# Second attention with two sets of buffers and its rolls in a row; MLP that rounds a pair behind the next pair's shrinking

## The chip, the cores and the metric

The kernel runs on one core of a Trainium2 chip. The metric is the device time of one execution in microseconds (us), median of three runs. TensorE is called PE below, VectorE DVE, ScalarE ACT, GpSimd POOL, and SyncE, which issues all transfers here, SP.

## What is computed

Two layers on `x` (32 batches x 64 tokens x 128), with `ctx` of the same shape as context. Each layer adds a gated attention and a gated MLP to the residual, each behind a layer norm. `setup_inputs` draws everything in float32.

```python
x = x + tanh(g_xattn[0]) * attention0(_layernorm(x), ctx)    # rope, 16 heads of 8, softmax
x = x + tanh(g_ffn[0]) * experts(_layernorm(x))              # 8 experts, top 2 for each batch of (8, 256), gelu
x = x + tanh(g_xattn[1]) * autocorrelation(_layernorm(x), ctx)
x = x + tanh(g_ffn[1]) * fp4_mlp(_layernorm(x))

# autocorrelation, for each batch
Q, K, V = (query @ Wq + bq), (key @ Wk + bk), (value @ Wv + bv)       # split in heads
corr = irfft(rfft(Q) * conj(rfft(K)))
w, idx = top_k(corr.mean(axis=-1), 4)                                 # the best four lags of a head
out = sum over the four: softmax(w) * V rolled by idx                 # then @ Wo + bo

# fp4_mlp: blocks of 16 are scaled by max(abs)/6, rounded to the fp4 grid, scaled back
h = silu(fp4_linear(x, w_gate)) * fp4_linear(x, w_up)                 # 352 wide
return fp4_linear(h, w_down)                                          # quantises h and w_down too
```

## The kernel before, in words

**Tiling.** `x` stays in SBUF as 16 tiles (`TILES`) of 128 rows (two batches) x 128 columns. A group is four tiles, so there are four groups (`G4`); a pair is two tiles, so there are eight pairs (`PAIRS`). All intermediate data lies in one large SBUF tensor, `region`, which every stage carves anew, so in the trace nearly every operand is called `s_region`. PSUM is one tensor `ps` of eight banks.

**What sets the order.** There is no scheduler. Each engine has one hand-written list of calls (`@block.vector` and its fellows), and semaphores, named in `names`, make it wait. The order of work on an engine is the order of the calls in the text, and an instruction that waits holds everything behind it on its engine.

**Stages.** The first attention runs to about 93 us; routing and experts follow to 171 us; the second attention to its last residual add at 214 us, with its output product, the layer norm and the first quantisation to 229 us; the MLP then runs to 291.5 us. `keep_clock(n, bank)` (L1107) is `n` matmuls on PE whose result nobody reads.

**First attention.** For each tile, `keys_queries` makes the scores of two banks, `row_max` and `subtract` on DVE (L733, L741) and the exponent on ACT (L511) make the probabilities, PE turns them (L1143), ACT copies them (L516), PE multiplies by the values (L1156). A product of the output bias (PE L1197 and L1198, then DVE L764 into `bout`) stands between the loads of the pipeline and its loop.

**Second attention.** Two halves `k` of 16 batches each. Their heads' products of spectra (`products`, DVE L908) are summed by PE into bank 4 + k (`sum_heads`, L1363), copied by ACT (`sums_read`, L597), turned by PE (`turn_sums`, L1374), copied by ACT (`sums_turned`, L603), and transformed back by PE (`correlate`, L1382). DVE finds the best lags (`best_lags`, L910 to L929, with an exponent on ACT, L607, in its midst), PE turns them (`turn_lags`, L1413), ACT spreads them over the heads (`turn_gx`, L614). For each pair of tiles, PE makes the spectrum of the roll (`spectrum`, L1424), and DVE multiplies it with the spectrum of the values (`roll_values`, L938). `context_kv(n)` (L1244, with a small bias product L1230) projects keys (n below 4) and values (n from 4); ACT copies them (L534). `cfs`, `cfT`, `gx`, `y1` and the bank of the correlation have one buffer each, so the second half waits for the first at each of them. Spectra use two banks:

```python
if q >= 2:
    pe.wait_ge(m["of_done"], 2 * (q - 1))
```

`out_product` (L1432), `y1_turned` (ACT L619), `out_tokens` (L1439) and `attention_out` (DVE L969) end the stage for each group; `turn_weights` (PE L1324, L1328; copy ACT L587) turns the quantised weights of the MLP in between.

**MLP.** A group of `x` is quantised in five steps: `x_scale` (DVE: reduce, scale, reciprocal, shrink, L268 to L270 and L275), `x_magnitude` (ACT L667), `x_round` (DVE L279, twice), `x_unscale` (POOL L286, 512 columns), `turn_x` (PE L1472) with its copy (ACT L650). A pair then goes through `gate_up` (PE L1485), `silu` (ACT L655), the product `hh` (DVE L995), reduce (L1005), scale (L1010), reciprocal (L1011), shrink (L275), `magnitude` (ACT L661), the rounding (DVE L279, 704 columns, twice), the unscaling (POOL L286, 704 columns), `turn_h` (PE L1499), its copy to `hT` (ACT L688), `down` (PE L1509) and `finish` (DVE L1017, the residual add). In `pair_step(q)` DVE does the product of pair q, the rounding of pair q-1, the reduce of pair q, `finish(q - 3)`, then scale, reciprocal and shrink of pair q. PE's loop is:

```python
for q in range(PAIRS + 2):
    if q + 1 < PAIRS:
        gate_up(q + 1)
    if q >= 2:
        down(q - 2)
    if 1 <= q <= PAIRS:
        turn_h(q - 1)
```

with `turn_x` at its end for q of 0, 2 and 4.

## Time and profile before

| what | us |
|---|---|
| median of three runs (297.94 to 299.8) | 299.23 |
| the profiled execution, its own time | 295.81 |
| its span in the trace | 293.8 |
| outside the span (the difference) | 2.0 |

The profile is of one execution. Its span is the time from the first to the last recorded instruction or transfer; the device time holds some 2.0 us more. A row of a timeline gives the start, the duration, the engine, the line, the operation, what it writes and reads, the shape, how many instructions the row stands for, and in brackets how long the engine had been idle before and what released it. The granted clock of PE is given as a share of its full speed (in the 40 slices in tenths, in the windows as a mean).

### The profile page before, as it was taken

Reading aid. Unit: us, or ns where it says so; the run is one execution under the profiler, and the core shown is the slowest. Engines: PE = TensorE matmul, PEld = TensorE weight load, DVE = VectorE, ACT = ScalarE, POOL = GpSimd, SP = SyncE. Lnnn points to the kernel's source line nnn. Section 1 sums busy time; section 2 is a strip of 40 time slices with the busy share of each in tenths; the row PEclk is TensorE's granted clock in tenths of the full one; section 3 lists DMA queues with packets and bytes.
Section 4 is the critical chain, followed back from the end, with each engine's and each line's share of the span. In section 5 each row is a group of like instructions: output and inputs, shape, how many; then the busy total and the mean of one; then the engine's idle time right before and its main releaser. Section 6 shows DMA issues by size and latency. Waiting matters only on the chain.

```text
span 293.8 us, 6298 instructions
## 1 busy us (share of the span) xinstructions
PE 261.2 (89%) x2190; PEld 203.5 (69%) x2190; DVE 199.5 (68%) x538; ACT 161.4 (55%) x368; POOL 120.8 (41%) x172
## 2 busy tenths in 40 slices
PE   8999899999899999999999998987857869696955
PEld 5655466666578789999999975554645547374855
DVE  3997588889987744322222269746287999998981
ACT  2579975555786666666666647224443824443421
POOL 4573879995203042299522015302253131313121
PEclk9999999999999999999999999999998969797999
DMA  7997000000001197767777300000000000000001
GB/s 204 370 363 316 3 2 0 2 2 2 2 3 20 73 379 325 294 287 288 288 289 300 134 0 2 1 3 0 0 0 0 2 1 0 18 19 19 18 19 56
DMA packets 12159, 30.15 MB, mean 103 GB/s; under 512 B 992, under 2 KB 5216, under 8 KB 12000
## 3 DMA queue, kind: packets, MB, share of 16 engines
q1 hardware_dynamic: 12128, 29.75, 26.8%
q8 instruction: 18, 0.29, 0.4%
q14 instruction: 13, 0.11, 0.1%
HBM read 9.75 MB, written 1.05 MB: 37 GB/s over the span
## 4 chain that ended last, share of the span: by engine, by line
PE 63%; DVE 17%; ACT 7%; issue 5%; POOL 3%; DMA 2%; SPq 1%; DVEq 0%; ACTq 0%; POOLq 0%
PE ps L1307 11%; PE ps L1296 11%; PE ps L1156 5%; PE ps L1130 4%; PE ps L1485 4%; PE ps L1143 4%; DVE s_region L279 4%; PE ps L1058 3%; PE ps L1424 3%; PE ps L1049 2%; DVE s_small L228 2%; PE ps L1166 2%; PE ps L1050 2%; DVE s_region L995 2%; DVE s_small L1005 1%
## 5 line engine op out<-in xcount | busy, mean ns | idle before, releaser
L573 ACT ACTIVATE s_region<-ps,s_region 128x128 f32<-128x128 f32 x144 | 41.1, 369 | 22.0 <-PE ps L1296 21.8
L868 DVE SCALAR_TENSOR_TENSOR s_ctxT<-ps,s_region,s_ctxT 128x64 f32 x72 | 18.1, 282 | 44.3 <-PE ps L1307 44.2
L1296 PE MATMUL ps<-s_region 128*128 128x128 f32 x288 | 38.5, 276 | 0.3
L1307 PE MATMUL ps<-s_region 128*128 128x128 f32 x288 | 37.9, 275 | 0.0
L286 POOL TENSOR_TENSOR s_region<-s_region,s_small 128x704 f32<-128x704 f32 (+2 forms) x13 | 17.5, 1343 | 46.5 <-DVE s_region L279 46.5
L1296 PEld LDWEIGHTS ps<-s_region 128*128 128x128 f32 x288 | 35.0, 192 | 1.0 <-DMA s_region<-s_wall 0.6
L1307 PEld LDWEIGHTS ps<-s_region 128*128 128x128 f32 x288 | 35.0, 192 | 0.2 <-issue 0.2
L251 POOL TENSOR_TENSOR s_small<-s_small,s_par 128x4 f32<-128x4 f32 (+3 forms) x14 | 15.5, 1107 | 43.2 <-DVE s_small L234 43.2
L1485 PE MATMUL ps<-s_region 128*128 128x352 f32 x64 | 26.4, 570 | 2.3 <-ACT s_region L650 2.3
L398 POOL COPY s_region<-s_xt 128x64 f32 x72 | 14.8, 238 | 32.1 <-PE ps L1296 22.0
L733 DVE TENSOR_REDUCE s_small<-ps 128x16 f32<-128x1024 f32 x16 | 19.6, 1225 | 9.9 <-PE ps L1130 9.9
L516 ACT COPY s_region<-ps 128x512 f32<-128x512 f32 x32 | 17.2, 588 | 16.3 <-PE ps L1143 16.2
L345 POOL TENSOR_SCALAR s_region<-s_region 128x512 f32<-128x512 f32 x16 | 24.7, 1572 | 2.1 <-PE ps L1130 2.1
L242 ACT ACTIVATE s_xn<-s_x,s_small 128x128 f32<-128x128 f32 x47 | 19.5, 485 | 5.4 <-POOL s_small L253 5.3
L279 DVE SCALAR_TENSOR_TENSOR s_region<-s_region 128x704 f32<-128x704 f32 (+1 forms) x24 | 20.6, 859 | 2.6 <-ACT s_region L667 1.2
L1485 PEld LDWEIGHTS ps<-s_region 128*128 128x128 f32 x64 | 14.2, 234 | 11.0 <-issue 4.0
L741 DVE TENSOR_TENSOR s_region<-ps,s_small 128x1024 f32<-128x1024 f32 x16 | 18.7, 1171 | 0.0
L1156 PEld LDWEIGHTS ps<-s_region 128*64 128x64 f32 x512 | 16.2, 138 | 3.1 <-ACT s_region L516 1.5
L1156 PE MATMUL ps<-s_region 128*64 128x18 f32 x512 | 17.8, 212 | 0.3 <-ACT s_region L516 0.2
L511 ACT ACTIVATE s_region<-s_region 128x1024 f32<-128x1024 f32 x16 | 17.1, 1068 | 1.3 <-DVE s_region L741 1.2
L1130 PE MATMUL ps<-s_region 64*64 64x512 f32 x128 | 17.4, 614 | 0.0
L1143 PE MATMUL ps<-s_par,s_region 128*128 128x128 f32 x128 | 16.6, 273 | 0.0
(216 smaller groups left out, 509.0 us busy)
## 6 DMA issues: line engine op xcount, KB each, us to landing
s_region<-s_wall SPq DMA_DIRECT2D x36, 514.0 KB, 3.0
s_wall<-wall SPq DMA_DIRECT2D x8, 514.0 KB, 9.0
s_par<-par SPq DMA_DIRECT2D x1, 1316.0 KB, 10.5
s_x<-x SPq DMA_DIRECT2D x2, 512.0 KB, 6.8
out<-s_x SPq DMA_DIRECT2D x8, 128.0 KB, 1.8
s_region<-ffn SPq DMA_DIRECT2D x1, 560.0 KB, 3.6
s_ctxT<-ctxT SPq DMA_DIRECT2D x2, 256.0 KB, 4.2
s_ctxT<-ctxT SPq DMA_DIRECT2D x1, 512.0 KB, 6.7
```

Of the source, the lines that this page charges most:

```text
L242: ins = eng.activation(xn[:, t, :], x[:, t, :], ACT.Identity, bias=shift[:, t:t + 1], scale=rstd[:, t:t + 1])
L279: return eng.scalar_tensor_tensor(out, mag, 1.5, z, ALU.max, ALU.subtract)
L345: pool.tensor_scalar(kbd[g % 2][:, j, :], cols, hmask[:, j:j + 1], None, ALU.mult).then_inc(m["kbd_done"], 1)
L573: ins = act.activation(hg[j % 3][:, c, :], ps[:, j % 3, RPT * S * c:RPT * S * (c + 1)], ACT.Gelu, bias=wbuf[j % 6][:, FF + FC * D + c:FF + ...
L733: dve.tensor_reduce(mx[t % 2], scores(t % 2), AX, ALU.max).then_inc(m["mx_done"], 1)
L741: dve.tensor_tensor(ssub[t % 2], scores(t % 2), mx[t % 2].unsqueeze(2).broadcast_to([P, H, S]), ALU.subtract).then_inc(m["s_sub"], 1)
L1130: ins = mm(ps[S * row:S * row + S, 2 * (t % 2) + half, :], qT[rows, 2 * t + row, :], kbd[g % 2][rows, :, k:k + S], start=True, stop=True)
L1143: ins = tr(ps[:, 4 + half, P * k:P * k + P], pr[t % 2][:, c:c + P], ident)
L1156: ins = mm(ps[S * row:S * row + S, 6 + t % 2, n * c:n * c + n], pT[t % 2][:, c, S * row:S * row + S], vbd[:, 2 * t + row, c, :], start=Tru ...
L1296: ins = mm(ps[:, j % 3, RPT * S * c:RPT * S * (c + 1)], w[:, P * c:P * c + P], xg[j % 4], start=True, stop=True)
L1307: ins = mm(ps[:, 4 + j % 2, 0:RPT * S], w[:, FF + D * c:FF + D * c + D], hg[j % 3][:, c, :], start=(c == 0), stop=(c == FC - 1))
L1485: ins = mm(ps[:, 1 + 2 * n + t, 0:MLP], xqT[(q // 2) % 2][:, lo:lo + P], wguT[:, MT * P * n:MT * P * n + MLP], start=True, stop=True)
```

## The change

**First attention.** The two matmuls of the bias product move on PE from ahead of the first turning of probabilities to a place behind the keys and queries of tile 2, and DVE's `bout` from ahead of `subtract(1)` to behind `row_max(2)`.

**Second attention.** `cfs`, `cfT`, `gx` and `y1` get a second buffer, the correlation a bank for each half (7 - k); turned sums and lags go to bank 4 + k. Spectra use four banks, so roll q waits for roll q-4. PE has both halves' sums, turns and correlations in a row; the values' projections 4 and 5 stand earlier (where `keep_clock` stood twice), 6 and 7 behind both correlations. `queries(3)` stands ahead of `sum_heads(0)`, `products(3)` ahead of the last two bias adds on DVE. ACT's order follows. POOL normalises two tiles of the last group and ACT two, instead of POOL four. The output product and the weights are turned at other places among the spectra.

**MLP.** DVE's `pair_step(q)` does product, reduce, `finish(q - 3)`, scale, reciprocal and shrink of pair q, and only then the rounding of pair q-1. PE's loop is now `down(q - 3)`, `gate_up(q + 1)`, `turn_h(q - 2)`, `turn_x`. ACT copies `hT` of pair q-2, where it was q-1. `finish` of the last three pairs stands behind the loop.

```diff
+KV_BANK = (6, 7, 6, 7, 6, 7, 2, 3)
+SPEC_BANK = (0, 1, 6, 7)
...
+        cfs = [carve(18432, 4, P), carve(8192, 4, P)]
+        cfT = [carve(18944 + 256 * i, 2, P) for i in range(2)]
...
+        gx = [carve(26880, TILES // 2, H, HD), carve(16384, TILES // 2, H, HD)]
...
+        y1 = [carve(27904, 4, P), carve(25600, 4, P)]
...
             sums_read(0)
+            sums_read(1)
             sums_turned(0)
-            kv_turned(4)
+            sums_turned(1)
             exp_lead(0)
-            sums_read(1)
-            sums_turned(1)
+            kv_turned(6)
             turn_gx(0)
-            kv_turned(5)
             exp_lead(1)
-            kv_turned(6)
+            kv_turned(7)
             turn_gx(1)
-            kv_turned(7)
...
-                if q >= 1:
-                    act.wait_ge(m["ht_done"], q)
-                    act.copy(hT[(q - 1) % 2].rearrange("p a k b -> p a (k b)"), ps[:, 5:7, 0:MT * P]).then_inc(m["ht_used"], 1)
+                if q >= 2:
+                    act.wait_ge(m["ht_done"], q - 1)
+                    act.copy(hT[q % 2].rearrange("p a k b -> p a (k b)"), ps[:, 5:7, 0:MT * P]).then_inc(m["ht_used"], 1)
...
             products(2)
+            products(3)
             bias_added(2)
             bias_added(3)
-            products(3)
...
-                if second:
-                    dve.wait_ge(m["hm_done"], q)
-                    dd.step(fp4_off(dve, hd[w], hm[w], hh[w].rearrange("p a n -> p (a n)")))
-                    fp4_off(dve, hd[w], hm[w], hd[w]).then_inc(m["hd_done"], 1)
-                if first:
...
-                if q >= 3:
-                    finish(q - 3)
-                if first:
+                    if q >= 3:
+                        finish(q - 3)
                     dd.after(k)
...
                     fp4_shrunk(dve, blocks(flat), blocks(flat), spread(hin[n3], 2 * NH)).then_inc(m["hv_done"], 1)
+                if 1 <= q <= PAIRS:
+                    dve.wait_ge(m["hm_done"], q)
+                    if q >= 3:
+                        dve.wait_ge(m["hq_done"], q - 2)
+                    dd.step(fp4_off(dve, hd[w], hm[w], hh[w].rearrange("p a n -> p (a n)")))
+                    fp4_off(dve, hd[w], hm[w], hd[w]).then_inc(m["hd_done"], 1)
...
-            keep_clock(4, 1)
+            context_kv(4)
             turn_experts(3)
             to_frequency(0)
-            keep_clock(3, 3)
+            context_kv(5)
...
+            queries(3)
             sum_heads(0)
-            queries(3)
-            context_kv(4)
+            sum_heads(1)
             turn_sums(0)
-            sum_heads(1)
+            turn_sums(1)
             correlate(0)
-            context_kv(5)
-            turn_sums(1)
             correlate(1)
+            context_kv(6)
+            context_kv(7)
...
-                if q >= 2:
-                    pe.wait_ge(m["of_done"], 2 * (q - 1))
+                if q >= 4:
+                    pe.wait_ge(m["of_done"], 2 * (q - 3))
+                elif q >= 2:
+                    pe.wait_ge(m["corr_read"], 2)
+                else:
+                    pe.wait_ge(m["pp_done"], 2 * G4)
...
-            for q in range(PAIRS + 2):
+            for q in range(PAIRS + 3):
+                if q >= 3:
+                    down(q - 3)
                 if q + 1 < PAIRS:
                     gate_up(q + 1)
-                if q >= 2:
-                    down(q - 2)
-                if 1 <= q <= PAIRS:
-                    turn_h(q - 1)
+                if 2 <= q <= PAIRS + 1:
+                    turn_h(q - 2)
+                if q in (0, 2, 4):
+                    turn_x(q // 2 + 1)
```

PE's order in the second attention, from the first turned lags on. L1413 turns lags, L1424 is a spectrum, L1244 with L1230 a projection of values. Before:

```order
L1413 MATMUL ps<-s_par,s_region 128x128 [waits hs_read,lags_ready]
L1424 MATMUL ps<-s_par,s_region 128x256 [waits gx_ready]
L1424 MATMUL ps<-s_par,s_region 128x256
L1424 MATMUL ps<-s_par,s_region 128x256 [waits gx_ready]
L1424 MATMUL ps<-s_par,s_region 128x256
L1413 MATMUL ps<-s_par,s_region 128x128 [waits cf_ready,lags_ready]
L1244 MATMUL ps<-s_region,s_par 128x512 [waits kv_used,cf_used]
L1230 MATMUL ps<-s_small,s_par 128x8 [waits bias64_ready]
L1424 MATMUL ps<-s_par,s_region 128x256 [waits of_done,gx_ready]
L1424 MATMUL ps<-s_par,s_region 128x256
L1424 MATMUL ps<-s_par,s_region 128x256 [waits of_done,gx_ready]
L1424 MATMUL ps<-s_par,s_region 128x256
```

The same place now (L1422 turns lags, L1437 is a spectrum, L1334 turns weights):

```order
L1422 MATMUL ps<-s_par,s_region 128x128 [waits cf_ready,lags_ready]
L1437 MATMUL ps<-s_par,s_region 128x256 [waits pp_done,gx_ready]
L1437 MATMUL ps<-s_par,s_region 128x256
L1437 MATMUL ps<-s_par,s_region 128x256 [waits pp_done,gx_ready]
L1437 MATMUL ps<-s_par,s_region 128x256
L1422 MATMUL ps<-s_par,s_region 128x128 [waits cf_ready,lags_ready]
L1437 MATMUL ps<-s_par,s_region 128x256 [waits corr_read,gx_ready]
L1437 MATMUL ps<-s_par,s_region 128x256
L1437 MATMUL ps<-s_par,s_region 128x256 [waits corr_read,gx_ready]
L1437 MATMUL ps<-s_par,s_region 128x256
L1334 MATMUL ps<-s_par,s_region 128x128 [waits kv_used,wq_ready]
```

The last projection of values is gone from between the spectra, and the third and fourth spectrum wait for `corr_read` (DVE has copied the second correlation) where they waited for `of_done` (DVE has multiplied the roll two before).

DVE's order in the MLP, `pair_step(3)` and the `x_scale(3)` behind it. L995 is the product, L279 with 704 columns the rounding of pair 2, L1005 the reduce, L1017 `finish(0)`, L275 a shrink. Before:

```order
L995 TENSOR_TENSOR s_region<-s_region,ps 128x704
L279 SCALAR_TENSOR_TENSOR s_region<-s_region 128x704 x2
L1005 TENSOR_REDUCE s_small<-s_region 128x44
L1017 SCALAR_TENSOR_TENSOR s_x<-ps,s_small,s_x 128x256
L1010 TENSOR_SCALAR s_small<-s_small 128x44
L1011 RECIPROCAL s_small<-s_small 128x44
L275 SCALAR_TENSOR_TENSOR s_region<-s_region,s_small 128x704
L268 TENSOR_REDUCE s_small<-s_xn 128x32
```

Now, from the end of `pair_step(2)` and the `x_round(2)` behind it to the same `x_scale(3)` (L999 is the product, L281 the rounding, L1004 the reduce, L1021 `finish`, L277 the shrink, L270 the first step of `x_scale`):

```order
L281 SCALAR_TENSOR_TENSOR s_region<-s_region 128x704 x2
L281 SCALAR_TENSOR_TENSOR s_region<-s_region 128x512 x2
L999 TENSOR_TENSOR s_region<-s_region,ps 128x704
L1004 TENSOR_REDUCE s_small<-s_region 128x44
L1021 SCALAR_TENSOR_TENSOR s_x<-ps,s_small,s_x 128x256
L1008 TENSOR_SCALAR s_small<-s_small 128x44
L1009 RECIPROCAL s_small<-s_small 128x44
L277 SCALAR_TENSOR_TENSOR s_region<-s_region,s_small 128x704
L281 SCALAR_TENSOR_TENSOR s_region<-s_region 128x704 x2
L270 TENSOR_REDUCE s_small<-s_xn 128x32
```

Between the product and `finish` there were three instructions and there is one; a rounding of 704 columns now stands directly ahead of each `x_round` (512 columns) and each `x_scale`.

PE's order in the MLP around the `turn_x(3)` (L1472) of loop step 4. L1485 is `gate_up`, L1509 `down`, L1499 `turn_h`. Before:

```order
L1509 MATMUL ps<-s_region 128x128 x6
L1499 MATMUL ps<-s_par,s_region 128x128 x2
L1499 MATMUL ps<-s_par,s_region 96x128
L1499 MATMUL ps<-s_par,s_region 128x128 x2
L1499 MATMUL ps<-s_par,s_region 96x128
L1472 MATMUL ps<-s_par,s_region 128x128 x4
L1485 MATMUL ps<-s_region 128x352 x4
L1509 MATMUL ps<-s_region 128x128 x6
```

The same place now (L1482 is `turn_x`, L1519 `down`, L1495 `gate_up`, L1509 `turn_h`):

```order
L1509 MATMUL ps<-s_par,s_region 128x128 x2
L1509 MATMUL ps<-s_par,s_region 96x128
L1509 MATMUL ps<-s_par,s_region 128x128 x2
L1509 MATMUL ps<-s_par,s_region 96x128
L1482 MATMUL ps<-s_par,s_region 128x128 x4
L1519 MATMUL ps<-s_region 128x128 x6
L1495 MATMUL ps<-s_region 128x352 x4
```

Behind `turn_x` comes `down` first and then `gate_up`, where `down` followed `gate_up`.

## Rows read from the trace of the kernel before

**Rows 1.** The page: busy time of each engine.

```profile
PE 261.2 (89%) x2190; PEld 203.5 (69%) x2190; DVE 199.5 (68%) x538; ACT 161.4 (55%) x368; POOL 120.8 (41%) x172
```

**Rows 2.** Windows in the MLP: length, busy PE, PEld, DVE, ACT, POOL; clock, DMA.

```profile
229.00:243.00 14.00, 10.66 (x35) 6.60 (x34) 13.25 (x22) 7.03 (x13) 3.50 (x4) 0.78 0.01 2
...
257.00:271.00 14.00, 11.18 (x56) 8.07 (x55) 13.45 (x21) 5.11 (x9) 3.84 (x3) 0.87 0.07 20
```

**Rows 3.** Timeline of DVE in the second attention, where it waits.

```profile
193.26 0.29 DVE L913 COPY s_region<-ps 128x128 f32<-128x128 f32 x1 [2.14 <-PE ps L1382]
...
197.45 0.29 DVE L913 COPY s_region<-ps 128x128 f32<-128x128 f32 x1 [1.47 <-PE ps L1382]
...
200.41 0.29 DVE L924 SCALAR_TENSOR_TENSOR s_region<-s_region 128x128 f32<-128x128 f32 x1 [1.41 <-ACT s_region L607]
...
204.00 1.62 DVE L938 TENSOR_TENSOR s_region<-ps,s_region 128x256 f32<-128x256 f32 x4 [1.12 <-PE ps L1424]
207.15 1.62 DVE L938 TENSOR_TENSOR s_region<-ps,s_region 128x256 f32<-128x256 f32 x4 [1.53 <-PE ps L1424]
212.61 1.62 DVE L938 TENSOR_TENSOR s_region<-ps,s_region 128x256 f32<-128x256 f32 x4 [3.84 <-PE ps L1424]
```

**Rows 4.** Timelines of ACT and PE at the lags of the second half.

```profile
204.85 1.01 ACT L614 COPY s_region<-ps 128x1024 f32<-128x1024 f32 x1 [4.07 <-PE ps L1424]
...
202.78 1.97 PE L1424 MATMUL ps<-s_par,s_region 128*128 128x256 f32 x8
```

**Rows 5.** Timeline of DVE in the MLP: two pairs whole, and single rows around.

```profile
232.75 0.19 DVE L1010 TENSOR_SCALAR s_small<-s_small 128x44 f32<-128x44 f32 x1
...
249.24 1.41 DVE L279 SCALAR_TENSOR_TENSOR s_region<-s_region 128x512 f32<-128x512 f32 x2
250.57 0.88 DVE L995 TENSOR_TENSOR s_region<-s_region,ps 128x704 f32<-128x704 f32 x1
251.37 2.10 DVE L279 SCALAR_TENSOR_TENSOR s_region<-s_region 128x704 f32<-128x704 f32 x2
...
254.18 0.47 DVE L1017 SCALAR_TENSOR_TENSOR s_x<-ps,s_small,s_x 128x256 f32<-128x256 f32 x1
254.57 0.40 DVE L1010 TENSOR_SCALAR s_small<-s_small 128x44 f32<-128x44 f32 x1
...
259.01 1.81 DVE L279 SCALAR_TENSOR_TENSOR s_region<-s_region 128x704 f32<-128x704 f32 x2
...
264.97 0.88 DVE L995 TENSOR_TENSOR s_region<-s_region,ps 128x704 f32<-128x704 f32 x1
...
271.97 0.89 DVE L995 TENSOR_TENSOR s_region<-s_region,ps 128x704 f32<-128x704 f32 x1 [1.21 <-PE ps L1485]
...
283.92 1.82 DVE L279 SCALAR_TENSOR_TENSOR s_region<-s_region 128x704 f32<-128x704 f32 x2 [0.86 <-ACT s_region L661]
```

**Rows 6.** Timeline of POOL beside them.

```profile
250.73 1.06 POOL L286 TENSOR_TENSOR s_region<-s_region,s_small 128x512 f32<-128x512 f32 x1 [2.84 <-DVE s_region L279]
253.54 1.39 POOL L286 TENSOR_TENSOR s_region<-s_region,s_small 128x704 f32<-128x704 f32 x1 [1.75 <-DVE s_region L279]
```

**Rows 7.** Timeline of PE in the MLP.

```profile
245.12 2.53 PE L1485 MATMUL ps<-s_region 128*128 128x352 f32 x8
247.49 1.50 PE L1509 MATMUL ps<-s_region 128*128 128x128 f32 x12
...
251.85 0.66 PE L1472 MATMUL ps<-s_par,s_region 128*128 128x128 f32 x4 [2.20 <-POOL s_region L286]
253.18 4.33 PE L1485 MATMUL ps<-s_region 128*128 128x352 f32 x8 [0.68 <-ACT s_region L650]
```

**Rows 8.** Timeline of ACT in the MLP: the copy to `hT`, and `x_magnitude`.

```profile
250.06 0.78 ACT L688 COPY s_region<-ps 128x768 f32<-128x768 f32 x1
...
258.33 0.63 ACT L667 ACTIVATE s_region<-s_region 128x512 f32<-128x512 f32 x1 [1.14 <-DVE s_region L275]
```

**Rows 9.** Timeline of DVE in the first attention.

```profile
33.86 0.35 DVE L764 TENSOR_SCALAR s_region<-ps,s_small 128x128 f32<-128x128 f32 x1 [0.60 <-PE ps L1198]
```

More of the change, by code:

```diff
@@ L678, in _ @@
             normalise(act, 12, 16, m["xn_d"], 14)
-            for q in range(PAIRS + 1):
+            for q in range(PAIRS + 2):
                 if q + 1 < PAIRS:
@@ L990, in pair_step @@
                 u, w, n3 = q % 2, (q - 1) % 2, q % 3
-                first, second = q < PAIRS, 1 <= q <= PAIRS
-                if first:
+                if q < PAIRS:
                     dve.wait_ge(m["sg_done"], q + 1)
@@ L1029, in _ @@
             x_scale(1)
-            for q in range(PAIRS + 3):
+            for q in range(PAIRS + 1):
                 pair_step(q)
@@ L1035, in _ @@
                     x_scale((q + 3) // 2)
+            for q in range(PAIRS - 3, PAIRS):
+                finish(q)
         @block.tensor
@@ L1202, in _ @@
                     keys_queries(t + 2)
+                if t == 0:
+                    bias_product()
                 if t >= 1:
@@ L1525, in _ @@
                     keep_clock(9 if q == PAIRS - 2 else 3, 0)
-                if q in (0, 2, 4):
-                    turn_x(q // 2 + 1)
 def _constants():
```

107 lines of the change are left out of this document (52 added, 55 removed).

## The prediction

> **What bounds the kernel now.** I read the busy time of the engines first, then timelines of one engine after the other in the two stages that the change touches, then windows for the clock. PE is busy for 89% of the span and DVE for 68% [rows 1], but a share over the whole span says little: each stage has its own limit.
>
> In the second attention the thing to see is that DVE, at the end of the chain, waits six times: 2.14 and 1.47 us for the two correlations, 1.41 us for an exponent on ACT, and 1.12, 1.53 and 3.84 us for spectra [rows 3]. The last comes from one buffer: ACT's spreading of the second half's lags waits 4.07 us for the first half's spectra to be read, and PE's four spectra for it start only then [rows 4]. Latency bounds this stage, and buffers cause much of it.
>
> In the MLP the reverse holds. From the product at 250.57 to the one at 264.97, two pairs and 14.40 us, DVE has no gap [rows 5]; it is busy for 13.45 of 14 us while PE is busy for 11.18 [rows 2]. DVE bounds it. Two details matter. PE waits 2.20 us for POOL at L1472 and 0.68 us more for ACT, and then its `gate_up` takes 4.33 us where it takes 2.53 at other times [rows 7]; the granted clock over such stretches is 0.78 and 0.87 [rows 2], so part of them ran at 1.2 GHz and not 2.4, after a wait. DVE hides that today, with only 1.21 us of wait at one product [rows 5]. And POOL's unscaling of a pair takes 1.39 us and ends at 254.93; DVE's tiny L1010 began at 254.57 and ended at 254.97, taking 0.40 us where it takes 0.19 with POOL idle; the rounding beside POOL's other unscaling took 2.10 us, not 1.81 [rows 5, 6]. DVE and POOL get in each other's way.
>
> **First attention.** The bias product leaves the place ahead of the second subtraction. DVE waited 0.60 us and worked 0.35 us for it there [rows 9]; moved one tile later, its product is long there. PE does both matmuls anyway. What can come out is at most about 0.5 us and at least 0 (if PE, which does the same work, bounds the loop); I take -0.25, near L764's own time.
>
> **Second attention.** The removed and the shortened waits, one by one. The first correlation: both halves' sums now stand ahead of it on PE, but the bias adds leave DVE's path; I take no gain, since they cancel by about 1 us each. The second correlation comes right behind the first, so its 1.47 us go. The exponent is asked for earlier and stands only behind one spreading of 1.01 us: of 1.41 us about 0.4 stay, -1.0. The rolls' 1.12 + 1.53 + 3.84 = 6.49 us shrink, because four banks let PE run ahead and the second `gx` has its own buffer. What stays is PE's pace: four spectra for two rolls, 1.97 us [rows 4], against 1.62 us of DVE [rows 3], four times, some 0.35 x 4 = 1.4, and 0.3 for the first; about 1.7 stay, -4.8. Sum -1.5 - 1.0 - 4.8 = -7.3. The output products and weight turns now lie between the spectra, and the first tokens are ready a bit later relative to the last roll: +0.8, an estimate out of PE's order. Net -6.5. From both sides: none of the rolls' gain would leave -1.7, and every one of the six waits gone would be -11.5; the value is nearest to the rows that one buffer explains.
>
> **MLP, per two pairs.** The new order has DVE do product, reduce, `finish`, scale, reciprocal, shrink of pair q and only then the rounding of q-1. No instruction is added or dropped. Terms for the cycle of 14.40 us [rows 5]:
>
> - DVE and POOL meet elsewhere. The L1010 of both pairs get 0.40 - 0.19 = 0.21 us back, and one rounding 2.10 - 1.81 = 0.29: -0.71.
> - POOL's unscaling of 1.39 us [rows 6] starts when a rounding ends, and the next on DVE is now an `x_round` or an `x_scale`. The first instruction of an `x_round` (half of 1.41 us, rows 5) starts at once, its second has to wait for what remains of the 1.39: I take +1.3; behind `x_scale`, whose first instruction reads one buffer, the scaling of the middle is late by about half of POOL's time, +0.7. The bounds are 0 (they pass each other, as the product and POOL's 512-column unscaling of 1.06 us do [rows 5, 6]) and 1.39 each.
> - `finish(q - 3)` waits for `down(q - 3)`. It is still in the same place, but `down` now is issued an iteration later and `hT` is copied an iteration later, so `finish` has only the product and the reduce ahead of it, some 1.7 us. For even pairs `down` (1.50 us, rows 7) stands on PE behind `turn_x`, which waits for POOL's 1.06 behind POOL's 1.39 [rows 6]; then 1.06 + 0.66 + 1.50 = 3.2 us stand against that cover of 1.7: +1.5. For odd pairs ACT's copy of 0.78 us stands behind `x_magnitude` of 0.63 us [rows 8]; 0.63 + 0.78 + 1.50 = 2.9 against 1.7: +1.25. The bounds are 0 (down is issued in time) and 3.2 each.
>
> Sum 14.40 - 0.71 + 2.0 + 2.75 = 18.4, that is +4.0 per two pairs. It applies once in full, for the pairs 3 and 4. Pairs 0 to 2 have no `finish` yet: of the above only the meeting with POOL, +0.7. Pairs 5 and 6 have no `x_scale`, and the wait of 1.21 us at their product [rows 5] covers part: 2.75 - 1.21 - 0.42 = +1.1. For pair 7 and the end there are two waits of about 1.3, less the 0.86 us that DVE stood for ACT's magnitude [rows 5] and that a rounding now covers, less 0.2 at L1010: +1.5. After the last rounding the chain is the same as before. Sum 0.7 + 4.0 + 1.1 + 1.5 = +7.3.
>
> What is queued behind a waiting `finish`: scale, reciprocal and shrink of pair q on DVE, so ACT's magnitude, and the rounding of q-1, so POOL, `turn_h` and the next `down`. It is a loop: a late `down` makes the next one late. This is why the waits add up.
>
> The Trainium skill, page "SBUF — State Buffer", section "SBUF: two separate sides", states that the port pair DVE and GpSimd share is an exclusive lock, held for a whole instruction by whoever starts first, where DVE's instruction has two SBUF inputs and GpSimd's reads SBUF. The trace agrees: L1010 ended 0.04 us behind POOL's 1.39 us. By that rule the second half of `x_round` and of the later roundings meets a lock held since a rounding ended, as in the term above, and speaks against this order; by the reading that they pass each other the sum would be 2.0 us lower in the full cycle.
>
> **The clock.** PE's waits in the MLP are 2.20 + 0.68 us before a slow `gate_up` [rows 7]. In the new order `turn_x` waits for both unscalings and `down` for `finish`, so I estimate waits of 4 to 5 us. A slow `gate_up` costs 4.33 - 2.53 = 1.80 us and a slow `down` as much as it lasts, 1.5. Before, DVE hid it; now `down` and `gate_up` stand on the path. One and a half such misses is +2.5; the bounds are 0 and, for three slow `gate_up` with nothing to hide them, 3 x 1.80 = 5.4. The Trainium skill, page "TensorE: Matmul & The Clock Gate", section "HAM oscillation — how this bites in real kernels", says that waits between groups of matmuls put TensorE back to half its clock each time, so that every group starts cold; that is the third rival below. By that rule each `turn_x` wait here costs a slow `gate_up`, as the trace shows after 2.20 us already.
>
> **Sum.** -0.25 - 6.5 + 7.3 + 2.5 = +3.05. The profiled execution took 295.81 us, of which 293.8 are its span and 2.0 lie outside, which nothing here changes: 295.81 + 3.05 = 298.86. The median of the runs is 299.23, 3.42 above the profiled one, so 302.3 on its scale.
>
> **Rivals.**
>
> - An even exchange: the attention gives 6.75 and the MLP takes 7.3, but the clock is as before. Speaks for it: most of PE's work is the same, only in another order, and PE waited before too. Against: its waits grow. +0.55, 299.8.
> - The rolls' gain stands and `finish` never waits: faster. The mechanism is in one place, L1017: `down(q - 3)` stands first in PE's loop, and if PE comes to it while DVE still does the shrink of the pair before, `dn_done` is there when DVE asks. It decides when `turn_h` and its copy are done before the product of pair q. Then in the MLP only the meeting with POOL stays, 0.7 + 2.0 - 0.71, less the freed 1.21 and 0.86: about -0.1, and the time is 299.23 - 6.75 - 0.1 = 292.4. For it: DVE has no gap now at any L1017 in the two pairs [rows 5]. Against: the cover is 1.7 us where a rounding of 1.81 to 2.10 us more stood before.
> - The clock stays low over most of the MLP: the clock term is 5.4 + 0.4 for the first `gate_up` and not 2.5, +3.3 more, 305.6. For it: 0.78 in the first stretch [rows 2].
> - The rolls don't run in a row: the copies of the last values (ACT) or the exponent hold the second `gx`, and the attention gives only 3.3: 302.3 + 3.2 = 305.5. Against: ACT waits 4.07 us there and has room [rows 4].
>
> **How the numbers follow.** The forecast 0.42, the even exchange 0.22, the faster case 0.14, the low clock 0.14, the rolls 0.08. About 1%, 3 us, is what a measurement of this kernel can tell from no change. The forecast, at +3.1, lies on the bound and is split between slower and same, 0.25 and 0.17; the even exchange is same but for 0.02 faster; the two last are slower. Slower 0.25 + 0.14 + 0.08 = 0.47, same 0.17 + 0.20 = 0.37, faster 0.14 + 0.02 = 0.16. The range leaves out most of the faster case. Its low end is the forecast without the clock term (2.5), without the meetings with POOL (2.7) and without 1.7 of the waits, 295.4; its high end is the case of the low clock, 305.6, with 1.4 us more of waits for `down`, 307.0. The forecast's own range is 300 to 305.
>
> **What would show it.** In the profile after: the copy of the second correlation (L913 of before) without a wait, four rows of rolls with waits under 1 us, the last rolls some 7 us earlier than 212.61 [rows 3]; in the MLP, waits of 1 to 1.5 us at the `finish` on PE's `down`, an `x_round` of about 2.5 us where it is 1.41, and windows with a clock under 0.87. Wrong would be: no wait at `finish`; products in the MLP 14.4 us apart per two pairs; or a clock of 1.00.

## The result

The changed kernel takes 302.25 us (median of 4 runs, 302.03 to 302.51) against 299.47 us for the kernel before in the same measurement: ratio 1.0139, 95% interval 1.0089 to 1.019. A second measurement on another occasion gave 301.27 against 297.49 us, ratio 1.0131 (1.0071 to 1.0192). It is slower by somewhat over 1%: 2.8 us in the first measurement and 3.8 in the second, where +3.05 was forecast.

The profiled execution after took 302.03 us, its span is 299.9. Its page:

```profile
PE 261.0 (87%) x2176; PEld 205.0 (68%) x2176; DVE 201.9 (67%) x538; ACT 162.2 (54%) x370; POOL 120.6 (40%) x170
```

Only DVE is busy for longer than before, 201.9 us where it was 199.5 [rows 1]; the others are within 1.5 us. Most of the 6.1 us by which the span grew is waits. The clearest reading is by three marks: the first residual add of layer 1 (L896 before, L899 after), the last roll, and the first product of the MLP, with the end of the last residual add. Timeline of DVE, these marks before (the last roll stands in [rows 3]):

```profile
172.67 0.75 DVE L896 SCALAR_TENSOR_TENSOR s_x<-ps,s_small,s_x 128x512 f32<-128x512 f32 x1 [0.84 <-PE ps L1336]
...
230.91 0.89 DVE L995 TENSOR_TENSOR s_region<-s_region,ps 128x704 f32<-128x704 f32 x1 [0.23 <-PE ps L1485]
...
291.04 0.48 DVE L1017 SCALAR_TENSOR_TENSOR s_x<-ps,s_small,s_x 128x256 f32<-128x256 f32 x1 [2.67 <-PE ps L1509]
```

And after (the last roll and the first product stand in the next fence):

```profile
174.21 0.75 DVE L899 SCALAR_TENSOR_TENSOR s_x<-ps,s_small,s_x 128x512 f32<-128x512 f32 x1 [0.84 <-PE ps L1346]
...
297.17 0.48 DVE L1021 SCALAR_TENSOR_TENSOR s_x<-ps,s_small,s_x 128x256 f32<-128x256 f32 x1 [2.67 <-PE ps L1519]
```

| | first add | last roll | first product | end of last add | MLP's length |
|---|---|---|---|---|---|
| before | 172.67 | 212.61 | 230.91 | 291.52 | 60.6 |
| after | 174.21 | 207.14 | 228.25 | 297.65 | 69.4 |
| difference | +1.5 | -5.5 | -2.7 | +6.1 | +8.8 |

So up to the first add 1.5 us are lost, from there to the last roll 7.0 are won, from the last roll to the first product 2.8 are given back, and in the MLP 8.8 are lost.

**Second attention.** Timeline of DVE, the rows that answer to [rows 3], and the first product:

```profile
195.18 0.29 DVE L916 COPY s_region<-ps 128x128 f32<-128x128 f32 x1 [2.39 <-PE ps L1391]
...
197.82 0.28 DVE L916 COPY s_region<-ps 128x128 f32<-128x128 f32 x1
...
199.65 0.29 DVE L927 SCALAR_TENSOR_TENSOR s_region<-s_region 128x128 f32<-128x128 f32 x1 [0.30 <-ACT s_region L605]
...
202.46 1.62 DVE L941 TENSOR_TENSOR s_region<-ps,s_region 128x256 f32<-128x256 f32 x4 [0.22 <-PE ps L1437]
204.52 1.62 DVE L941 TENSOR_TENSOR s_region<-ps,s_region 128x256 f32<-128x256 f32 x4 [0.44 <-PE ps L1437]
207.14 1.62 DVE L941 TENSOR_TENSOR s_region<-ps,s_region 128x256 f32<-128x256 f32 x4 [1.00 <-PE ps L1437]
...
228.25 0.89 DVE L999 TENSOR_TENSOR s_region<-s_region,ps 128x704 f32<-128x704 f32 x1 [1.04 <-PE ps L1495]
```

The second correlation waits for nothing, the exponent's wait is 0.30 where it was 1.41, and the rolls' waits are 0.22, 0.44 and 1.00, together 1.66 where they were 6.49. This is the forecast for these waits one by one (0, 0.4, 1.7).

**MLP.** Timeline of DVE, pairs 3 to 5 and the wait of pair 7, which answers to [rows 5]:

```profile
238.69 0.87 DVE L271 TENSOR_SCALAR s_small<-s_small 128x32 f32<-128x32 f32 x1
...
243.93 4.21 DVE L281 SCALAR_TENSOR_TENSOR s_region<-s_region 128x704 f32<-128x704 f32 x4
248.05 0.87 DVE L999 TENSOR_TENSOR s_region<-s_region,ps 128x704 f32<-128x704 f32 x1
249.03 0.89 DVE L1004 TENSOR_REDUCE s_small<-s_region 128x44 f32<-128x704 f32 x1
253.03 0.48 DVE L1021 SCALAR_TENSOR_TENSOR s_x<-ps,s_small,s_x 128x256 f32<-128x256 f32 x1 [3.12 <-PE ps L1519]
...
262.91 0.48 DVE L1021 SCALAR_TENSOR_TENSOR s_x<-ps,s_small,s_x 128x256 f32<-128x256 f32 x1 [1.77 <-PE ps L1519]
...
268.93 0.88 DVE L999 TENSOR_TENSOR s_region<-s_region,ps 128x704 f32<-128x704 f32 x1
...
272.23 0.48 DVE L1021 SCALAR_TENSOR_TENSOR s_x<-ps,s_small,s_x 128x256 f32<-128x256 f32 x1 [1.44 <-PE ps L1519]
...
284.13 0.48 DVE L1021 SCALAR_TENSOR_TENSOR s_x<-ps,s_small,s_x 128x256 f32<-128x256 f32 x1 [0.89 <-PE ps L1519]
```

From the product of pair 3 to that of pair 5 it is now 20.88 us, where it was 14.40 [rows 5]. `finish` (L1021) waits 3.12, 1.77, 1.44 and 0.89 us for `down`, where it waited for nothing before. In this document the wait at `finish` "of pair q" is the one in `pair_step(q)`, which adds pair q-3; these four are of the pairs 3, 4, 5 and 7. Behind the loop the last two adds wait 3.00 and 2.67 us (1.76 and 2.67 before). Timelines of PE and, last, POOL say why:

```profile
220.78 2.05 PE L1451 MATMUL ps<-s_region,s_par 128*128 128x512 f32 x2 [3.64 <-DVE s_x L974]
222.62 1.78 PE L1116 MATMUL ps<-s_par 128*128 128x128 f32 x8
...
249.32 1.11 PE L1482 MATMUL ps<-s_par,s_region 128*128 128x128 f32 x4 [5.64 <-POOL s_region L288]
250.23 2.77 PE L1519 MATMUL ps<-s_region 128*128 128x128 f32 x12
...
260.76 2.12 PE L1519 MATMUL ps<-s_region 128*128 128x128 f32 x12 [3.76 <-ACT s_region L690]
...
238.14 1.39 POOL L288 TENSOR_TENSOR s_region<-s_region,s_small 128x704 f32<-128x704 f32 x1 [4.00 <-DVE s_region L281]
245.82 1.77 POOL L288 TENSOR_TENSOR s_region<-s_region,s_small 128x704 f32<-128x704 f32 x1 [6.29 <-DVE s_region L281]
```

`turn_x` waits 5.64 us for POOL (2.20 before, [rows 7]), and `down` behind it takes 2.77 us and not 1.50, at the lower clock. L271, ahead in the fence of DVE, begins at 238.69 and ends at 239.56; POOL's instruction ends at 239.53. At the next meeting POOL's own instruction takes 1.77 us and not 1.39. The windows, to be set against [rows 2]:

```profile
229.00:243.00 14.00, 10.45 (x44) 7.45 (x43) 13.45 (x22) 5.64 (x10) 2.45 (x2) 0.88 0.01 2
243.00:257.00 14.00, 8.36 (x37) 6.50 (x35) 10.57 (x15) 3.50 (x5) 3.01 (x3) 0.76 0.03 9
257.00:271.00 14.00, 7.10 (x33) 5.38 (x34) 11.57 (x16) 3.66 (x6) 4.03 (x3) 0.88 0.03 9
```

The granted clock is no lower than before: the three windows have a mean of 0.84, and so have those of before (0.78, 0.87 and 0.87). What is new is that DVE falls to 10.57 and 11.57 us of 14: PE's slow stretches have come out from behind DVE. How much of the loss they are, the experiments have to say. One part of the diff has no words ahead: the idle matmuls of loop step 0 stood ahead of `turn_x` and now stand behind it. The products of pairs 1 and 2 wait for nothing, so it costs DVE nothing.

### The profile page after: what moved, and what is told of

It is laid out like the page before. It is cut to its first block, busy times and chain, and to the rows that moved or that the text cites. A ratio compares the mean times of both kernels' runs of the same rounds, so it can differ in the third digit from the quotient of the medians.

```text
span 299.9 us, 6276 instructions
## 1 busy us (share of the span) xinstructions
PE 261.0 (87%) x2176; PEld 205.0 (68%) x2176; DVE 201.9 (67%) x538; ACT 162.2 (54%) x370; POOL 120.6 (40%) x170
## 3 DMA queue, kind: packets, MB, share of 16 engines
HBM read 9.75 MB, written 1.05 MB: 36 GB/s over the span
## 4 chain that ended last, share of the span: by engine, by line
PE 61%; DVE 13%; issue 10%; ACT 7%; POOL 4%; DMA 2%; SPq 1%; DVEq 0%; POOLq 0%
PE ps L1317 11%; PE ps L1306 10%; PE ps L1162 5%; PE ps L1136 4%; PE ps L1149 4%; POOL s_region L288 3%; PE ps L1519 3%; PE ps L1064 3%; PE ps L1437 2%; DVE s_region L281 2%; PE ps L1055 2%; PE ps L1172 2%; PE ps L1056 2%; PE ps L1354 2%; PE ps L1451 1%
## 5 line engine op out<-in xcount | busy, mean ns | idle before, releaser
L288 POOL TENSOR_TENSOR s_region<-s_region,s_small 128x704 f32<-128x704 f32 (+2 forms) x13 | 18.8, 1444 | 53.5 <-DVE s_region L281 53.5
L1306 PEld LDWEIGHTS ps<-s_region 128*128 128x128 f32 x288 | 35.0, 192 | 1.1 <-DMA s_region<-s_wall 0.7
L1317 PEld LDWEIGHTS ps<-s_region 128*128 128x128 f32 x288 | 35.0, 192 | 0.2 <-issue 0.2
L281 DVE SCALAR_TENSOR_TENSOR s_region<-s_region 128x704 f32<-128x704 f32 (+1 forms) x24 | 22.7, 955 | 2.1 <-ACT s_region L669 1.7
L1495 PE MATMUL ps<-s_region 128*128 128x352 f32 x64 | 23.1, 511 | 0.2 <-ACT s_region L652 0.2
L244 ACT ACTIVATE s_xn<-s_x,s_small 128x128 f32<-128x128 f32 x49 | 20.4, 485 | 3.9 <-POOL s_small L255 3.8
L1519 PE MATMUL ps<-s_region 128*128 128x128 f32 (+1 forms) x96 | 14.4, 306 | 7.8 <-ACT s_region L690 7.8
L1519 PEld LDWEIGHTS ps<-s_region 128*128 128x128 f32 (+1 forms) x96 | 13.1, 215 | 8.7 <-ACT s_region L690 8.7
L1495 PEld LDWEIGHTS ps<-s_region 128*128 128x128 f32 x64 | 13.2, 220 | 7.3 <-issue 2.5
L1136 PE MATMUL ps<-s_region 64*64 64x512 f32 x128 | 18.1, 637 | 0.0
```

The lines of the kernel that those rows point to most:

```text
L244: ins = eng.activation(xn[:, t, :], x[:, t, :], ACT.Identity, bias=shift[:, t:t + 1], scale=rstd[:, t:t + 1])
L281: return eng.scalar_tensor_tensor(out, mag, 1.5, z, ALU.max, ALU.subtract)
L288: return eng.tensor_tensor(blocks(out), blocks(diff), spread(sc, nblk), ALU.mult)
L1136: ins = mm(ps[S * row:S * row + S, 2 * (t % 2) + half, :], qT[rows, 2 * t + row, :], kbd[g % 2][rows, :, k:k + S], start=True, stop=True)
L1306: ins = mm(ps[:, j % 3, RPT * S * c:RPT * S * (c + 1)], w[:, P * c:P * c + P], xg[j % 4], start=True, stop=True)
L1317: ins = mm(ps[:, 4 + j % 2, 0:RPT * S], w[:, FF + D * c:FF + D * c + D], hg[j % 3][:, c, :], start=(c == 0), stop=(c == FC - 1))
```

## The experiments

The first four share their runs of the kernel before (median 297.88 us), as do the next four (299.04) and the last four (297.49).

**The kernel before once more.** No edit.

> 

> The kernel before, unchanged, for the clock and span of each execution and a second profile. Theory: the profiled execution of 295.81 us was one without a stretch at 1.2 GHz in the first attention (the profile after has one, at 77 to 81 us, of 1.6 us), and most executions have one or two more; so most spans lie near 297 us at a mean clock below 0.971, and the second profile shows one such stretch outside the MLP. Rival: the clock of all executions is 0.971 and the spread has another cause.

Measured: 298.11 us, ten executions from 295.63 to 299.94, spans 293.6 to 297.8 at mean clocks of 0.977 down to 0.963. So the theory holds in its main part: the profiled execution of 295.81 us was among the quickest, and the longer executions have the lower mean clock. The mean clock is not all of the spread: among all executions of this kernel on record, those with a mean of 0.971 have spans from 293.5 to 297.9 us. The second profile (295.89 us) is again one without a slow stretch in the first attention, so it could not show it; a later run does. Another one shows a slow stretch that the granted clock does not show. Timeline of PE in the run of `finish` later:

```profile
5.37 2.05 PE L1055 MATMUL ps<-s_ctxT,s_par 128*128 128x512 f32 x2 [0.61 <-DMA s_ctxT<-ctxT]
7.21 1.91 PE L1056 MATMUL ps<-s_ctxT,s_par 128*128 128x512 f32 x2
```

In the first profile of the kernel before the two groups take 1.10 and 1.02 us. Two of the 14 profiles lose over 2 us here, at a recorded clock of 1.00; whether it is the clock all the same stays open.

**The bias product alone.** The part of the diff in the first attention.

```diff
             for t in range(TILES):
                 turn_probs(t)
                 if t + 2 < TILES:
                     keys_queries(t + 2)
+                if t == 0:
+                    bias_product()
```

> 

> The bias product of the first attention moved alone. Theory: the scores of tile 3 come 0.4 us earlier, so 299.1 us, within 1% of the kernel before. Rival: the slow stretch of the clock at 77 us comes with the move, +1.6 - 0.4 = +1.2, so 300.7 us, in the profile and in every execution.

Measured: ratio 0.999 (0.9933 to 1.0047). From the scores of tile 1 to those of tile 3 it is 6.35 us here and 6.77 before: -0.42. No slow stretch came with the move in the first attention, so the rival falls. This profile has one in the second attention instead. Timeline of PE:

```profile
200.99 3.78 PE L1429 MATMUL ps<-s_par,s_region 128*128 128x256 f32 x8 [1.10 <-ACT s_region L614]
```

The group takes 1.99 us in the kernel before, behind the same wait of 1.10 us, and from the first add to the last roll it is 42.5 us here and 39.9 there.

**Both attentions, the MLP of before.**

```diff
-            for q in range(PAIRS + 3):
-                if q >= 3:
-                    down(q - 3)
+            for q in range(PAIRS + 2):
                 if q + 1 < PAIRS:
                     gate_up(q + 1)
...
+                if q >= 2:
+                    down(q - 2)
...
```

(and the rest of PE's loop, `pair_step` and ACT's loop as before)

> 

> The changes of both attentions, with the MLP of the kernel before. Theory: -0.25 - 6.5 with the clock as before, so 292.7 us. Rival: the last output product of the second attention and its keep_clock now run at 1.2 GHz ahead of the first turn_x, 1.6 us on the path as in the profile after, so the gain at the first product of the MLP is about 5 us, 294.5 us. A second rival: DVE bounds the MLP only if it is fed, and half of the gain goes in it: 296 us.

Measured: 293.02 us, ratio 0.9814 (0.9707 to 0.9921). The time is near the theory's 292.7, but only because the kernel before is quicker in this measurement: the gain is 4.9 us, and that is the first rival's. In this profile, too, the last output product and what follows it are slow, and the first product (228.34) waits 1.59 us for `gate_up`. The MLP's length is 60.5 us as before, so it takes the earlier start without loss; the second rival falls.

**The MLP alone.** The reverse: the kernel before with

```diff
-                if 1 <= q <= PAIRS:
-                    turn_h(q - 1)
+                if 2 <= q <= PAIRS + 1:
+                    turn_h(q - 2)
```

and the rest of the MLP's part of the diff.

> 

> The MLP's change alone, with the attentions of the kernel before. Theory: +7.3 for waits and meetings with POOL and +2.5 for the clock, so 309.3 us; waits of over 1 us at the finish of pairs 3 and 4. Rival: the MLP's loss is only a loss of clock by where the attention ends in time, and alone it costs under 4 us, under 303.5 us.

Measured: 307.93 us, ratio 1.0333 (1.0219 to 1.0447), MLP's length 70.5 us; `finish` waits 3.12, 1.93, 1.88, 1.20 and 0.89 us. The loss belongs to the MLP's order by itself (+10.1 us, where +9.8 was expected). Its profile also shows what the kernel before can do, since up to the MLP it is that kernel. Timeline of PE:

```profile
76.47 0.33 PE L1163 MATMUL ps<-s_par,s_region 128*128 128x128 f32 x1 [1.05 <-DVE s_region L750]
...
78.19 1.59 PE L1144 MATMUL ps<-s_par,s_region 128*128 128x128 f32 x8
79.71 1.99 PE L1131 MATMUL ps<-s_region 64*64 64x512 f32 x8
```

After a wait of 1.05 us the two groups that take 1.04 and 1.09 us elsewhere take 1.59 and 1.99. The same stretch is slow in the profile after, which is its 1.5 us up to the first add, and it does not need the change: it is slow in 7 of the 14 profiles of this study, one of the three with the old order of the first attention and six of the eleven with the new. Whether the new order makes it more frequent, these counts can't tell.

**`finish` later.**

```diff
-                    if q >= 3:
-                        finish(q - 3)
                     dd.after(k)
...
                     fp4_shrunk(dve, blocks(flat), blocks(flat), spread(hin[n3], 2 * NH)).then_inc(m["hv_done"], 1)
+                    if q >= 3:
+                        finish(q - 3)
```

> 

> The changed kernel with finish(q - 3) behind the shrink of pair q (it stood ahead of the scale), so that scale, reciprocal and shrink, 1.5 us, cover its wait too. Theory (finish waits for a late down and holds the pair): the waits of 3.12, 1.77, 1.44 and 0.89 us shrink by up to 1.5 us each, about 4 us in all, 298.2 us. Rival (PE's queue is late for other reasons and the wait only shows it): the wait is found again at the next product or rounding, 302 us.

Measured: 296.61 us, ratio 0.9953 (0.9908 to 0.9999), the MLP's length 64.0 us and not 69.4. Timeline of DVE, the only waits at `finish` ahead of the last two:

```profile
253.68 0.48 DVE L1021 SCALAR_TENSOR_TENSOR s_x<-ps,s_small,s_x 128x256 f32<-128x256 f32 x1 [1.51 <-PE ps L1519]
...
281.54 0.48 DVE L1021 SCALAR_TENSOR_TENSOR s_x<-ps,s_small,s_x 128x256 f32<-128x256 f32 x1 [0.45 <-PE ps L1519]
```

Each wait is shorter by the cover or gone: 3.12 to 1.51, 1.77 and 1.44 to 0, 0.89 to 0.45, together 5.3 us, and that is what the MLP is shorter by (about 4 us were expected). The wait at `finish` was on the path in full; the rival falls.

**`x_round` and `x_scale` ahead of the rounding.**

```diff
+                if q in (0, 2, 4):
+                    x_round(q // 2 + 1)
+                if q in (1, 3):
+                    x_scale((q + 3) // 2)
                 if 1 <= q <= PAIRS:
                     dve.wait_ge(m["hm_done"], q)
```

(and both calls taken from behind `pair_step(q)`)

> 

> The changed kernel with x_round and x_scale ahead of the rounding of the pair, so that none of them begins together with POOL's 1.39 us. Theory: x_round falls from about 2.4 to 1.4 us and x_scale's L271 from 0.87 to 0.18 us, four places, -3.3 us; the roundings stand 1.3 to 2 us later, and down with them, which gives back up to half: 300.5 us. Rival (the meeting only moves to the rounding, and its lateness goes straight into the waits at finish): 302 to 304 us.

Measured: 301.8 us, ratio 1.0142 (1.0061 to 1.0222): no gain. Timeline of DVE:

```profile
236.73 0.18 DVE L271 TENSOR_SCALAR s_small<-s_small 128x32 f32<-128x32 f32 x1
...
243.86 3.14 DVE L281 SCALAR_TENSOR_TENSOR s_region<-s_region 128x512 f32<-128x512 f32 x4
...
253.15 0.48 DVE L1025 SCALAR_TENSOR_TENSOR s_x<-ps,s_small,s_x 128x256 f32<-128x256 f32 x1 [4.36 <-PE ps L1519]
...
270.06 0.48 DVE L1025 SCALAR_TENSOR_TENSOR s_x<-ps,s_small,s_x 128x256 f32<-128x256 f32 x1 [2.78 <-PE ps L1519]
```

Both meetings with POOL are gone (0.18 for 0.87, 3.14 for 4.21), so their cause and size are shown: 3.5 us in four places. Against it, the waits at `finish` go from 3.12 to 4.36 and from 1.44 to 2.78, while that of pair 4 (1.77) is gone: +0.8 in all. The product of pair 2 waits 0.77 us behind a slow `gate_up`, and the last two adds wait 4.33 and 3.06 us and not 3.00 and 2.67, the first behind a `down` of 2.77 us. So what is given back is in part the later rounding and in large part slow groups of PE, which no run here separates. The rival is about right as to the time; the meeting did not move to the rounding, which keeps its 1.81 us.

**Idle matmuls in PE's waits, many.**

```diff
+                if 0 <= q <= 4:
+                    keep_clock((16, 8, 32, 20, 20)[q], 0)
                 if q in (0, 2, 4):
                     turn_x(q // 2 + 1)
```

> 

> The changed kernel with 96 more idle matmuls on PE in the MLP, ahead of turn_x and at the ends of the loop steps 0 to 4, where PE waits. Theory (clock): the MLP's windows show a clock near 1.00, down takes 1.50 us and not 2.77 and 2.12, the waits at finish of pairs 3 and 4 fall to about 1.4 and 1.1 us; -2.5 us or a little more, 299.7 us. Rival (the clock is hidden as before the change, or the idle matmuls delay turn_x by as much): 302 us.

Measured: 299.13 us, ratio 1.0024 (0.9984 to 1.0064), executions from 297.8 to 301.7. The clock in the MLP is 1.00, `down` takes 1.50, and yet `finish` of pair 3 waits 2.90 us, since the idle matmuls ran over. Each call of `keep_clock` counts as two matmuls in the trace. Timelines of PE and of DVE:

```profile
243.93 7.31 PE L1116 MATMUL ps<-s_par 128*128 128x128 f32 x64
251.08 0.60 PE L1482 MATMUL ps<-s_par,s_region 128*128 128x128 f32 x4
...
253.06 0.48 DVE L1021 SCALAR_TENSOR_TENSOR s_x<-ps,s_small,s_x 128x256 f32<-128x256 f32 x1 [2.90 <-PE ps L1519]
```

Counted from the first product, `turn_x` starts 1.5 us later than in the profile after (22.60 and 21.07). The ratio is the theory's (299.7 expected), and the wait at pair 3 the rival's; a run with fewer decides.

**The same in the kernel with both attentions changed and the old MLP.**

```diff
                 if q in (0, 2, 4):
+                    keep_clock(16, 0)
                     turn_x(q // 2 + 1)
```

> 

> Both attentions changed, the MLP of the kernel before, and 16 idle matmuls ahead of each of its three later turn_x. Theory: DVE bounds this MLP except for the waits at products behind a slow gate_up (0.5 and 1.2 us in the profile of the kernel before), so at most -1.7 us against the same kernel without them: 291.5 to 293 us. Rival: the idle matmuls delay turn_x, and the time rises to 295 us.

Measured: 292.64 us, ratio 0.9816 (0.9724 to 0.9909), against 293.02 and 0.9814 without: the windows of its MLP show 1.00, and nothing measurable comes of it. The slow output product ahead of the MLP is still there.

**The changed kernel again.** No edit.

> 

> The changed kernel, unchanged, for more executions of it beside the kernel before. Theory: ratio between 1.01 and 1.02 as in the first measurement (302.25 us); the waits at finish of the pairs 3, 4 and 5 (3.1, 1.8 and 1.4 us) come again, also where the first attention has no slow stretch of the clock. Rival: the profile after had met a rare run of slow stretches, and the median falls to that of the kernel before.

Measured: 301.27 us, six executions from 300.24 to 303.11, ratio as given above; the waits at `finish` of pairs 3 to 7 are 2.94, 2.59, 1.44, 0 and 0.89 us. This profile has the slow stretch of the first attention too, so it does not show the waits without it.

**Idle matmuls, fewer.** `(13, 4, 22, 14, 12)[q]` in the edit above.

> 

> The changed kernel with 65 idle calls on PE in the MLP where e7_warm had 96, set to end before the operand of turn_x or down is there. Theory: down at 1.50 us and turn_x no later than in the changed kernel, so the wait at finish of pair 3 falls from 3.1 to 1.4 us, of pair 4 from 1.8 to 1.2 us; 2.3 us faster than the changed kernel, 300 us. Rival: the wait stays at 2.9 us as in e7_warm, then the clock was no part of it.

Measured: 298.98 us, ratio 1.0055 (1.0008 to 1.0101). Timelines of DVE and of PE:

```profile
249.09 0.48 DVE L1021 SCALAR_TENSOR_TENSOR s_x<-ps,s_small,s_x 128x256 f32<-128x256 f32 x1 [1.44 <-PE ps L1519]
...
258.45 0.48 DVE L1021 SCALAR_TENSOR_TENSOR s_x<-ps,s_small,s_x 128x256 f32<-128x256 f32 x1 [1.26 <-PE ps L1519]
...
264.46 0.88 DVE L999 TENSOR_TENSOR s_region<-s_region,ps 128x704 f32<-128x704 f32 x1
...
247.06 0.66 PE L1482 MATMUL ps<-s_par,s_region 128*128 128x128 f32 x4 [0.77 <-POOL s_region L288]
247.55 1.50 PE L1519 MATMUL ps<-s_region 128*128 128x128 f32 x12
```

This is the cycle without the clock: waits of 1.44 and 1.26 us, and 18.67 us from the product of pair 3 (245.79) to that of pair 5. The median is 2.3 us under the changed kernel's in the same measurement (301.27), as expected, and the rival falls. The run with 96 calls has the same median (299.13): what their overrun costs shows in its profile only.

**Both: `finish` later and the fewer idle matmuls.**

> 

> The idle calls of e10_warm_light and the late finish of e5_finish_late together. Theory: of the wait of 1.5 us that e5 still has at pair 3 nothing stays, so 1.5 us under e5_finish_late (296.6 us), 295 us, and what then is left against the attention's change alone (293.0 us) is what DVE and POOL cost each other: twice 1.0 and twice 0.7 us in the middle and 1.0 at the end. Rival: same as e5_finish_late.

Measured: 293.41 us, ratio 0.9847 (0.9772 to 0.9921), MLP's length 62.4 us, no wait at `finish` for pairs 3 to 6. That is quicker than expected (295), the rival falls, and it is still behind the old MLP with its clock kept (58.8, below).

**The old MLP, kept warm from the output product on.**

```diff
             out_product(3)
+            keep_clock(13, 7)
             out_tokens(3)
...
                 if q in (0, 2, 4):
+                    keep_clock(11, 0)
                     turn_x(q // 2 + 1)
```

> 

> Both attentions changed, the MLP of the kernel before, 11 idle calls ahead of each later turn_x and 13 ahead of the last output product of the second attention, where PE waits 3.6 us and then runs the product and the first turn_x at 1.2 GHz. Theory: the first product of the MLP comes 1.6 us earlier than in e8_attention_warm and DVE carries that to the end, 291.0 us. Rival: DVE's own work ahead of the MLP ends no earlier, and the time stays at 292.6 us.

Measured: 288.37 us, ratio 0.97 (0.9644 to 0.9755), the quickest version. Timelines of PE and DVE and two windows:

```profile
220.72 1.10 PE L1450 MATMUL ps<-s_region,s_par 128*128 128x512 f32 x2 [0.75 <-DVE s_x L974]
...
226.57 0.89 DVE L1000 TENSOR_TENSOR s_region<-s_region,ps 128x704 f32<-128x704 f32 x1 [0.23 <-PE ps L1495]
...
243.00:257.00 14.00, 11.24 (x66) 8.42 (x66) 13.67 (x22) 5.59 (x8) 3.51 (x3) 1.00 0.04 11
257.00:271.00 14.00, 13.13 (x89) 11.10 (x90) 13.66 (x22) 5.17 (x7) 4.16 (x4) 1.00 0.09 27
```

The output product takes 1.10 us (2.05 in the profile after), and the first product comes at 226.57 with 0.23 us of wait, where the run with 16 idle calls had 228.42 and 1.59. The MLP is 58.8 us long, 60.6 in the kernel before: the waits of 0.51 and 1.21 us at its products are gone. With 16 calls it was 59.9 and the product of pair 6 waited 1.05 us, so those had overrun. These two, 1.85 and 1.0 us, are the 2.8 us between the two spans (290.5 and 287.7). The medians lie 4.3 us apart (by the ratios, 3.5 us), and the profile still has the slow stretch of the first attention; five of the six executions have a mean clock of 0.998 or more, and why the stretch was rarer in them was not tried.

## Why the prediction was right, and where it was not

**The time.** 302.3 forecast, 302.25 measured, slower by 1.4%. That the two agree within 0.1 us is luck, since the kernel before alone spreads over 4 us. Between the two profiled executions the difference is 6.2 us and not 3.05: that of before was a quick one, 1.5 us of it by the slow stretch of the first attention that it did not have. The 3.42 us by which the sum was scaled to the median stand for such stretches in part.

**First attention, -0.25.** Measured -0.42 at tile 3, too small to see in the time.

**Second attention, -7.3 to the last roll.** Measured 7.0 (39.94 us from the first add to the last roll before, 32.93 after). Only the first correlation is off: it comes 0.4 us later behind the first add (20.97 us for 20.59), where no change was taken. Its wait is 2.39 us and not 2.14, and there is a seventh wait in this stage, which the forecast did not count: 1.89 us for PE at `products`, now 2.02.

**"+0.8, an estimate out of PE's order", from the last roll to the MLP.** This step failed: it is 2.8 us (18.30 before, 21.11 after). The run with the clock kept has 19.49, so 1.2 are the new order and 1.6 are the clock: PE waits 3.64 us for DVE and then does the output product and the idle matmuls slowly (2.05 and 1.78 us for 1.10 and 1.05), on the path. Before, the slow stretch lay one group earlier, where it was hidden: the third output product took 2.08 us and the add behind it waited for nothing. The forecast had put no clock term there. Net of the attentions: -4.2 in the profile, not -6.5.

**The MLP, +7.3 and the clock's +2.5.** Measured +8.8 together, by its parts:

| | pairs 0 to 2 | pairs 3 and 4 | pairs 5 and 6 | pair 7 and the end |
|---|---|---|---|---|
| forecast | +0.7 | +4.0, with the clock +6.5 | +1.1 | +1.5 |
| measured | +0.1 | +6.5 | 0.0 | +2.2 |

The middle is right. The forecast was too high in pairs 0 to 2, where it overlooked a wait of 0.51 us at the product of pair 2 and two L1010 of 0.68 us for 0.19, all of which went. In pairs 5 and 6 it counted two waits at `finish`, and that of pair 6 is none. At the end it left out that the roundings of pairs 6 and 7 now stand in a row and meet POOL: 4.60 us for the two, and the last instruction takes 1.96 us and not 0.88. Per two pairs without the clock 18.4 was forecast and 18.67 measured; the waits for `down` 1.5 and 1.25 forecast, 1.44 and 1.26 measured; `x_scale` +0.7, measured 0.69; `x_round` +1.3, measured 4.21 - 3.14 = 1.1, the second from the run in which it does not meet POOL. One more cost was left out: the reduce now follows its own product, 0.98 us from start to start where the pitch was 0.80 [rows 5], 0.4 in two pairs. By the rule of the Trainium skill ("SBUF — State Buffer", section "SBUF: two separate sides") that the shared ports are locked for a whole instruction by whoever starts first, the trace agrees: L271 ended 0.03 us behind POOL's. But L271 here and L1010 before read one buffer of SBUF and not two, so the case of two SBUF inputs that the prediction quotes is not theirs, and agreement on it can't be read from them; a second instruction of `x_round`, which reads two, is held in the same way (1.76 us for 0.7).

**The clock's term**, 2.5, was right in its place and near in its size: the waits at pairs 3 and 4 shrink by 3.12 - 1.44 = 1.7 and 1.77 - 1.26 = 0.5 when the clock is kept, together 2.2 (2.8 against the second profile of the changed kernel). Its reason was half wrong. The forecast saw longer waits and so more time at the lower clock; in fact the windows show nearly the same clock (0.88, 0.76, 0.88 against 0.78, 0.87, 0.87), and what changed is that DVE no longer hides it.

**That the terms add up** was wrong in one respect: the sum treats the meetings with POOL (2.0) and the waits for `down` (2.75) as separate. Taking the first away gave nothing, since waits of the same size came in their place. The attentions alone gave -4.9 us and the MLP alone +10.1, together +5.2, where the whole gave +2.8 and +3.8; the intervals of the two parts are over 3 us either way, so this speaks neither for nor against adding them.

**The rivals.** The even exchange (299.8) took the clock as it was before, hidden, and the run that keeps it at 1.00 gives 299.0. By parts it is less even: in that profile 4.6 us are won from the first add to the first product, not 6.5, and the MLP takes 6.7, not 7.3. The case that `finish` never waits (292.4) falls, but it named the right place, the cover at L1021: 1.5 us more cover give 5.4 back. The low clock over most of the MLP falls by the windows, and not each wait brought a slow group: behind 3.14 us at the last `turn_x`, `down` took 1.50 us and `gate_up` 2.53. The rolls did run in a row.

## What to carry to other kernels

When one engine bounds a stage without a gap, another engine's lateness costs nothing until a reordering takes the cover away; here two instructions less between a product and the residual add behind it put the latency of three other engines, and PE's slow clock, on the path. Place the instruction that may wait behind the work that others wait for, not ahead of it. Where TensorE runs at two clocks within a kernel, look for the waits ahead of a slow group on the path and fill them with work that ends before the operand is there.

## What the runs showed of the hardware that was not expected

The same stretch of the same program ran at the lower clock in some executions and not in others: after a wait of 1.02 to 1.06 us it was slow in 7 of 14 profiles and cost 1.5 to 1.6 us. Idle matmuls kept the granted clock at 1.00 in the MLP's windows from 229 to 271 us, where they filled the waits; where they overran by 1.5 us, the wait at `finish` was 2.90 us and not 1.44, about the 3.12 that it had been without them.

Of DVE's instructions beside POOL's 1.39 us only some were held: the scaling of 32 columns took 0.87 and not 0.18 us, and the second instruction of an `x_round` was held too, while the reduce of 512 columns ahead of the scaling kept its 0.68 us. POOL's own instruction, where it began beside the first instruction of that `x_round`, took 1.77 us.
